# Gate and up products in turn, and the low stationary operand second of three terms

## The reference

```
x = x + 0.5 * ffn(layernorm(x))
x = x + attn(layernorm(x))
x = x + 0.5 * ffn(layernorm(x))

ffn: scores = softmax(h @ gate_w.T)
     topk_w, topk_idx = top_k(scores.transpose(0, 2, 1), 256)   # per expert
     g = einsum('becd,efd->becf', x_tok, Wg)                    # F = 512
     u = einsum('becd,efd->becf', x_tok, Wu)
     eo = einsum('becf,edf->becd', gelu(g) * u, Wd) * topk_w    # scatter-added
     out + (gelu(h @ Ws_g.T) * (h @ Ws_u.T)) @ Ws_d.T           # shared expert
```

## Time and profile before

| | |
|---|---|
| Median of 3 runs | 1495.8 us (1495.22 to 1495.81) |
| Profiled execution, own time | 1495.36 us |
| Its span in the trace | 1493.6 us |
| TensorE busy | 1460.9 us, 98% |
| ScalarE, VectorE, GpSimd busy | 73%, 60%, 38% |
| Granted TensorE clock, mean | 0.998 of full speed |

### The profile page before, as it was taken

The page is one execution under the profiler, slowest core; times in us unless marked ns, Lnnn a source line. Parts: engine busy times, 40 slices in busy tenths (PEclk is TensorE's granted clock), DMA queues, the critical chain, the costliest instruction groups (busy, mean ns, idle before and its releaser), DMA issues. The chain is left out here.

```text
span 1493.6 us, 26824 instructions
## 1 busy us (share of the span) xinstructions
PE 1460.9 (98%) x9987; PEld 1025.7 (69%) x9987; DVE 893.9 (60%) x1985; ACT 1084.9 (73%) x1391; POOL 562.3 (38%) x485
## 2 busy tenths in 40 slices
PE   5999999999999999999999999999999999999998
PEld 4788888888997773333343343333788888888887
DVE  7888777777658971222144052126888867676774
ACT  7322277777746889999999999999622247777772
POOL 5000256666636961202111021110300046676645
PEclk9999999999999999999999999999999999999999
DMA  9212288888655798505336063221511158878873
GB/s 306 78 57 71 88 215 201 206 209 206 148 126 137 254 278 174 87 1 88 61 84 129 31 129 54 35 71 58 162 57 57 59 161 184 204 182 195 193 164 43
DMA packets 180403, 195.75 MB, mean 131 GB/s; under 512 B 77296, under 2 KB 142320, under 8 KB 177520
## 3 DMA queue, kind: packets, MB, share of 16 engines
q1 hardware_dynamic: 152096, 146.30, 39.1%
q0 software_dynamic: 28176, 47.73, 15.0%
HBM read 123.73 MB, written 55.57 MB: 120 GB/s over the span
## 5 line engine op out<-in xcount | busy, mean ns | idle before, releaser
L2497 ACT ACTIVATE 6426_pr<-6426_pS 128x1024 f32<-128x1024 f32 x448 | 420.5, 1196 | 2.0 <-PE 6426_pS L2392 2.0
L2423 PE MATMUL 6426_pO<-6426_pr,6411_vres 128*32 128x512 f32 x1792 | 237.3, 603 | 0.0
L2392 PEld LDWEIGHTS 6426_pS<-sq_rows,sk_rows 50*128 50x128 f32 x896 | 77.3, 183 | 177.8 <-ACT 6426_pr L2497 133.6
L2392 PE MATMUL 6426_pS<-sq_rows,sk_rows 50*128 50x512 f32 x896 | 183.4, 467 | 1.1 <-ACT 6426_prs L2497 0.8
L351 PE MATMUL 6437_pGU<-columns_ahead,weights_wts 128*128 128x512 f32 (+1 forms) x400 | 155.5, 389 | 1.1 <-DVE columns_ahead L1321 0.9
L2521 POOL TENSOR_SCALAR_AFFINE_SELECT 6426_pr<-6426_pr 128x512 f32<-128x512 f32 x32 | 20.3, 636 | 356.6 <-ACT 6426_pr L2497 356.6
L352 PE MATMUL 6437_pGU<-columns_ahead,weights_wts 128*128 128x512 f32 (+1 forms) x400 | 152.6, 382 | 0.0
L353 PE MATMUL 6437_pGU<-columns_ahead,weights_wts 128*128 128x512 f32 (+1 forms) x400 | 152.4, 381 | 0.0
L1120 ACT ACTIVATE hidden_hT<-6437_hf 128x512 fp32r<-128x512 f32 (+1 forms) x100 | 61.4, 614 | 107.7 <-DVE 6437_hf L1304 104.7
L1120 ACT ACTIVATE hidden_hT<-93_hf 128x512 fp32r<-128x512 f32 x96 | 60.6, 631 | 107.7 <-DVE 93_hf L1304 102.2
L1555 POOL DMA_INDIRECT out<-eo,6437_idx x64 | 106.6, 1665 | 78.7 <-issue 40.1
(11 more groups left out here) (445 smaller groups left out, 3754.9 us busy)
## 6 DMA issues: line engine op xcount, KB each, us to landing
93_raw_g<-WgT SPq DMA_DIRECT2D x16, 512.0 KB
93_raw_u<-WuT SPq DMA_DIRECT2D x16, 512.0 KB
93_raw_d<-WdT SPq DMA_DIRECT2D x16, 512.0 KB
q_rows<-rows_halves SPq DMA_DIRECT2D x8, 1024.0 KB, 4.8
k_rows<-rows_halves SPq DMA_DIRECT2D x8, 1024.0 KB, 5.1
6437_raw_g<-WgT SPq DMA_DIRECT2D x16, 512.0 KB
6437_raw_u<-WuT SPq DMA_DIRECT2D x16, 512.0 KB
6437_raw_d<-WdT SPq DMA_DIRECT2D x16, 512.0 KB
```

The lines of the kernel that those rows point to most:

```text
L2392: m = t_.matmul(to[:, e, :], key, query, start=True, stop=True)
L2423: m = t_.matmul(pO[e * 32:(e + 1) * 32, j % 2, off:off + wd], vres[:, (g // GB) * TPB + kt, at:at + 32], from_(e), start=n == first[j], st ...
L2497: s_exp.done(a.activation(to, pS[:, u % RING, :, :], ACT.Exp, scale=HD ** -0.5))
```

## The change

`product3` now issues its low stationary operand second and the low moving operand third. That holds for the down products, the projections and the attention's output as well. `gu` no longer calls it. It waits for the Gelu and for the product of block n - 2 at once, and then issues each of the six terms for gate and directly after for up: both read the same moving operand, with different stationary operands, and write different banks. The number of matmuls, their sizes, operands and banks stay. The hooks stay at the same count of matmuls within a block: (0, 1) is after six, (1, 0) after nine.

```diff
     def product3(self, pe, out, w_hi, w_lo, x_hi, x_lo, start, stop):
 
         pe.matmul(out, w_hi, x_hi, start=start, stop=False)
-        pe.matmul(out, w_hi, x_lo, start=False, stop=False)
-        return pe.matmul(out, w_lo, x_hi, start=False, stop=stop)
+        pe.matmul(out, w_lo, x_hi, start=False, stop=False)
+        return pe.matmul(out, w_hi, x_lo, start=False, stop=stop)
...
-                    for w, (ps, user, by) in enumerate(((pG, s_gelu, s_G), (pU, s_mul, s_U))):
-                        user.wait(t_, n - 1)
-                        for (k, cut), c in itertools.product(cuts, range(DC)):
-                            cols = slice(f * P, (f + 1) * P)
-                            m = self.product3(t_, ps(f % 2)[:, cut], weight(k, w, 0)[:, c, cols], weight(k, w, 1)[:, c, cols],
-                                              XT[0][:, col, c, cut], XT[1][:, col, c, cut], c == 0, c == DC - 1)
-                            if c == DC - 1 and cut == cuts[-1][1]:
+                    cols = slice(f * P, (f + 1) * P)
+                    s_gelu.wait(t_, n - 1)
+                    s_mul.wait(t_, n - 1)
+                    done = 0
+                    for (k, cut), c, (hw, hx) in itertools.product(cuts, range(DC), ((0, 0), (1, 0), (0, 1))):
+                        first_, last_ = (c, hw, hx) == (0, 0, 0), (c, hx) == (DC - 1, 1)
+                        for w, (ps, by) in enumerate(((pG, s_G), (pU, s_U))):
+                            m = t_.matmul(ps(f % 2)[:, cut], weight(k, w, hw)[:, c, cols], XT[hx][:, col, c, cut],
+                                          start=first_, stop=last_)
+                            if last_ and cut == cuts[-1][1]:
                                 by.done(m)
-                            if (w, c) in hook:
-                                side(s, hook[w, c])
+                            done += 1
+                            at = divmod(done // 3 - 1, DC)
+                            if done % 3 == 0 and at in hook:
+                                side(s, hook[at])
```

## The result

| | before | after |
|---|---|---|
| Median | 1495.52 us (1495.22 to 1495.81, 5 runs) | 1501.96 us (1500.95 to 1503.29, 5 runs) |
| Ratio | | 1.0043, 95% interval 1.0032 to 1.0054 |
| Profiled execution, own time | 1495.36 us | 1503.29 us |
| Its span | 1493.6 us | 1501.6 us |

The change costs 6.4 us (4.8 to 8.1 by the interval). I had forecast 3.9 us over this median, 1499.4 in a range of 1494 to 1504: the side is right and the time is in the range, the size is a good third too small. The profiled execution is the slowest of the five, 7.9 us over before's.

A forecast was written before the change was run, and what follows sets the result against it. TensorE, busy 98% of the span, bounds the kernel. Added waits 2.60 + 0.20 + 0.45 + 0.40 = 3.65 us on the profiled 1495.36 give 1499.0, with the median's 0.44 more 1499.4; range 1494 to 1504.

The forecast's parts named there:

- Pace, no gain taken: Gate and up matmuls on TensorE: 512-column starts stay 0.227 us apart, gain zero, bounds -10 and +20 us.
- Step 7, 2 x 1.30: Step 7, f = 0: block waits for VectorE's product, down products start 1.30 us later per feed-forward, 2.60 us in all.
- No second wait at f = 1: Step 7, next block: the product it needs ends at 144.33, before the block starts at 144.46, so no wait.
- Nothing takes it back: After step 7: token places, gathering and transposes hang on TensorE's later instructions, so the 1.30 us stays lost.
- Steps 1 and 2, 0.2 in all: Third block waits 0.6 us for the first's product, later count waits shrink; 0.1 kept per feed-forward, bounds 0 and 1.2.
- The last block, 0.45: End of first feed-forward: later Gelu delays the product and last down chunk by 0.45 us; second feed-forward covered.
- Steps 11 to 14 of the second feed-forward, 0.4: Planes parted about 1.1 us later, late product stalls a block 0.3 us, another 0.1; 0.4 taken, bounds 0 and 1.5.
- All other steps ... Cost nothing; if the cover went, each step would pay: Steady steps: product starts 0.4 to 0.6 us later, about 1.2 us of slack left, so no cost.
- The rival of the lag, 1508 at 0.12: Routed part: VectorE lags beyond 1.8 us, TensorE waits in most of 30 steps, 6 to 12 us more; 1508, chance 0.12.
- The rival that the waits are taken back: Slack behind step 7 absorbs the delay and small terms may vanish; 1496.2 to 1497.8, say 1497, chance 0.25.
- my sign for it: TensorE's wait for gathered columns shrinking by a microsecond would show the forecast wrong.

The follow-up runs named there:

- only the terms: Kernel before with only the order of the three terms changed in every product, gate and up keeping blocks and waits; -0.3 us over before, ratio 0.9998.
- both edges without the turn: Kernel before with both waits ahead of the block and gate told complete at the eleventh matmul, old matmul order; +6.0 and +7.4 us over before.
- step 7 undone alone: Changed kernel with the blocks of step 7 in both feed-forwards in their old form; +4.7 us over before, 2.5 us below the changed kernel.
- the early wait alone: Kernel before with both waits put ahead of a block's first matmul, six gate then six up; timed twice, +5.4 and +3.7 us over before.
- The timed experiment on all steps from 9 on: Changed kernel with the blocks of all steps from 9 on in their old form; +3.3 us over before, 3.9 us below the changed kernel.
- its second trace: The changed kernel run once more, unaltered, for a second trace; +7.2 us over the kernel before, ratio 1.0048.
- the early wait's second: Second run of the kernel before with both waits ahead of a block's first matmul; +3.7 us over before, ratio 1.0029.
- the late Gelu: Kernel before with gate told complete only at the eleventh of twelve matmuls, waits unmoved; +0.6 us over before, ratio 1.0004.

## Why the prediction was right, and where it was short

*Pace, no gain taken.* Right. 0.227 in the row of 24 matmuls; only the terms -0.3; both edges without the turn cost as much as the change. (The 215.8 ns that the prediction takes from the Trainium skill, "TensorE: Matmul & The Clock Gate", section "Back-to-back issue gap", is given there for an isolated matmul; for a stream of them with weight loads the same section has about 131 ns. The 227 ns here agrees with neither.)

*Step 7, 2 x 1.30.* The mechanism is right, the size 0.17 and 0.21 short: the block began 0.14 behind the product's end, and I had put 0.06, the distance in before; that is 0.08 of it, and the product itself came a little later. No second wait at f = 1, as forecast. "Nothing takes it back" holds for the change as it is, since step 9 is no less late than step 7's end; but with step 7 undone alone, only 0.9 and 1.0 came back by step 9.

*Steps 1 and 2, 0.2 in all.* 0.38.

*The last block, 0.45.* 0.44 and 0.45 in every trace with a late Gelu. For the second feed-forward I had the end covered, but its last item lost 0.29 at f = 2, with the early wait alone too. The row of the first now:

```profile
457.47 0.39 PE L351 MATMUL 93_pD<-columns_wts,hidden_hT 128*128 128x256 f32 x1 [0.46 <-DVE hidden_hT L1315]
```

*Steps 11 to 14 of the second feed-forward, 0.4, and "All other steps ... Cost nothing; if the cover went, each step would pay".* This is the step that was mis-sized. Steps 10 to 23 lost 2.37 + 0.82 = 3.2 us in the first trace against 0.4 forecast. The timed experiment on all steps from 9 on has 3.9, and its trace 3.0 by the starts of blocks, against 0.85 forecast for these steps with the last block. I knew the chain (join, queued work, Gelu of f = 2, product) and used it where the trace of before showed a late join, as if that landing belonged to that step. It doesn't: step 12 of the second feed-forward, where I had put 0.3, lost nothing. At the head of the chain of step 11 of the first, the time from the planes' end to the join was 7.0 us in before (no wait for the landing), 10.75 in the changed kernel, 8.0 in its second trace and 9.1 in the early wait's second. I had the later parting (1.1 us) right and used it in one place, where it acts in every step. I had also read the lag that may pass, 1.8, rightly, but compared it with the usual lag and not with the largest. What moves a landing by up to 3 us from one execution to the next stays open. Step 10, f = 0, pays 0.26 in each feed-forward because with the late Gelu the product of step 9, f = 2, is 1.89 late; ScalarE makes the turned columns ahead of that Gelu, which I hadn't gone through either.

*The rival of the lag, 1508 at 0.12*, had the right threshold and the wrong cause: not VectorE's load in 30 steps, but some 2 to 5 steps of 28 with a late transpose or gather.

*The rival that the waits are taken back* falls, though half of my sign for it came. The wait for the gathered columns in step 9 was to shrink by a microsecond and went from 0.95 to 0.39. TensorE in the down products ahead of it shows why that won nothing:

```profile
185.73 0.28 PE L352 MATMUL 93_pD<-weights_wts,hidden_hT 128*128 128x256 f32 x1 [0.59 <-issue]
...
187.95 0.73 PE L909 MATMUL 93_pGU<-columns_ahead,weights_wts 128*128 128x512 f32 x2 [0.39 <-DVE columns_ahead L1326]
```

The two together are 0.98, and step 9 began 1.84 late. I should have named the start of step 9 as the sign.

*The Trainium skill.* "Perfetto Trace Analysis", section "Matmuls", wants independent groups to rotate through banks so that the evacuation of one runs beside the matmuls of the next. The runs agree in this form: with the same banks, a gate reader released 1.13 us later and the up reader asked for 1.36 us earlier cost 6 us, and the order of matmuls alone nothing.

## What to carry to other kernels

A wait that is never reached in a trace is still slack in use, if something in the chain ahead of it varies: size it by the largest lag over several executions, not by the usual one. Here an edit left 1.7 of 3.1 us of cover, and lags of 1.8 to 4.3 us became stalls. Two edges that draw on the same slack are to be tried together: the late Gelu cost 0.6 alone; on top of the early wait it cost 0.6 in the first group of runs, and some 3 where the kernel before has 1495.5 to 1495.9 (+3.7 for the early wait, +6.4 and +7.2 for the change; not timed side by side). And interleaving two groups delays the first one's completion to nearly the end of both, for which the pace would have to give something back; here it gave nothing.

## What the runs showed that I had not expected

Alternating banks and reusing the moving operand up to four times in a row left the distance at 0.227 us to the last digit.

The kernel before had 1493.6 to 1493.7 us in some groups of runs and 1495.5 to 1495.9 in others. Chip number 0 stands in the record for a group of each kind, so the chip's number does not tell them apart. The traces of the first kind start step 9 of each feed-forward 12.60 us after the last matmul of step 8's blocks (read in the first feed-forward), those of the second kind 13.7 to 13.9. In these, VectorE and ScalarE start their rows just ahead of step 9 2.2 to 2.6 us further behind the same matmuls of TensorE, and TensorE itself often stops there for 0.4 to 0.7 us with no releaser named. That makes 2.2 to 2.6 us over both feed-forwards, about the difference in time. What causes it is open.

At the same place of the program (step 10 of the first feed-forward) the join began 7.0 to 10.75 us after the planes' end; in the traces where it waited for the transpose it was 7.4 to 10.75. The DMA engines were busy for 0.81 to 0.85 of the routed stretch. Which transfers it stood behind wasn't tried.
